# One reordered iteration and a row sent as runs, in a long-convolution and mixture kernel

## The reference, cut to what matters

```python
def cond(u, length, log_dt, C, log_A_real, A_imag, D):       # u is x: 64 batches, 64 heads, 1024 positions
    mask = (jnp.arange(Lq) < length[:, None]).astype(u.dtype)
    u_m = u * mask[:, None, :]
    dt = jnp.exp(log_dt); A = -jnp.exp(log_A_real) + 1j * A_imag
    dtA = A * dt[:, None]
    Cs = Cc * (jnp.exp(dtA) - 1.0) / A
    kernel = 2.0 * jnp.einsum('hn,hnl->hl', Cs, jnp.exp(dtA[:, :, None] * jnp.arange(Lq))).real
    y = causal_convolution(u_m, kernel) + u_m * D[:, None]   # by rfft and irfft of twice the length
    return y * mask[:, None, :]

def ffn(x, A, B, Wr):                                        # rows of 1024, 64 experts of rank 16
    scores = xf @ Wr.T
    top_vals, top_idx = jax.lax.top_k(scores, 16)
    G = zeros.at[rows, top_idx].set(jax.nn.softmax(top_vals, axis=-1))
    h = jnp.einsum('nd,krd->nkr', xf, A)
    return jnp.einsum('nkr,kdr->nd', h * G[:, :, None], B) * 2.0

out = x + ffn(cond(x, ...), A, B, Wr)
```

## Time and profile before

| what | value |
|---|---|
| median of 3 runs | 898.14 us (897.69 to 899.48) |
| the profiled execution | 898.15 us, span 896.3 us |
| TensorE busy | 881.5 us, 98% of the span |
| VectorE busy | 753.8 us, 84% |
| ScalarE busy | 371.6 us, 41% |
| chain that ended last | TensorE 91%, VectorE 4%, ScalarE 1%, DMA 1% |
| share of the 16 DMA engines, SyncE's queue | 42.1% |

### The profile page before, as it was taken

How to read it: one execution, slowest core, us unless ns; L and a number is a source line. 1 busy time by engine, 2 the same in 40 slices (tenths; PEclk the granted TensorE clock), 3 DMA queues, 4 the chain that set the end, 5 groups by cost and what they waited for, 6 DMA issues and landing times.

```text
span 896.3 us, 15701 instructions
## 1 busy us (share of the span) xinstructions
PE 881.5 (98%) x4488; PEld 783.0 (87%) x4488; DVE 753.8 (84%) x2580; ACT 371.6 (41%) x629; POOL 7.5 (1%) x24
## 2 busy tenths in 40 slices
PE   6999999999999999999999999999999999999998
PEld 4667998998899998899998889998889999889997
DVE  7899998888898888898888888888889888888722
ACT  5663554444542353543344443344453344442100
POOL 3000000000000000000000000000000000000000
PEclk9999999999999999999999999999999999999999
DMA  7631315444454444454433354434345444445331
GB/s 231 243 53 54 77 30 126 111 116 112 124 140 117 110 111 114 109 140 117 124 109 110 102 140 126 117 108 114 109 128 140 115 97 114 123 114 141 100 95 48
DMA packets 81415, 103.32 MB, mean 115 GB/s; under 512 B 30628, under 2 KB 63460, under 8 KB 81396
## 3 DMA queue, kind: packets, MB, share of 16 engines
q1 hardware_dynamic: 80868, 102.63, 42.1%
q0 software_dynamic: 160, 0.10, 0.2%
q10 hardware_dynamic: 368, 0.36, 0.1%
HBM read 67.34 MB, written 34.93 MB: 114 GB/s over the span
## 4 chain that ended last, share of the span: by engine, by line
PE 91%; DVE 4%; ACT 1%; issue 1%; DMA 1%; POOL 1%; SPq 0%; DVEq 0%; POOLq 0%; ACTq 0%
PE out_ps L1360 25%; PE h_ps L1360 18%; PE out_ps L1364 12%; PE h_ps L1364 9%; PE turn_ps L1360 8%; PE turn_ps L1364 4%; PE conv_ps L1316 2%; PE conv_ps L1317 2%; PE conv_ps L1318 2%; PE conv_ps L1289 1%; PE conv_ps L1326 1%; PE conv_ps L1290 1%; PE conv_ps L1327 1%; PE conv_ps L1328 1%; PE conv_ps L1291 1%; PE h_ps L1369 1%
## 5 line engine op out<-in xcount | busy, mean ns | idle before, releaser
L1360 PE MATMUL out_ps<-b_lo,g_hi 128*128 128x512 f32 x496 | 196.2, 395 | 0.0
L1360 PE MATMUL out_ps<-b_hi,g_hi 128*128 128x512 f32 x496 | 194.7, 393 | 0.0
L1360 PE MATMUL h_ps<-a_hi,y_hi 128*128 128x384 f32 x480 | 161.4, 336 | 0.0
L1360 PE MATMUL h_ps<-a_lo,y_hi 128*128 128x384 f32 x480 | 161.4, 336 | 0.0
L1364 PE MATMUL out_ps<-b_hi,g_lo 128*128 128x512 f32 x496 | 122.7, 389 | 0.3 <-DVE g_lo L1040 0.3
L564 ACT ACTIVATE g_hi<-square_sb 128x1024 fp32r<-128x1024 f32 x28 | 29.7, 1061 | 220.4 <-DMA square_sb<-moved 210.8
L1360 PEld LDWEIGHTS out_ps<-b_lo,g_hi 128*128 128x128 f32 x496 | 93.2, 188 | 21.2
L1364 PEld LDWEIGHTS out_ps<-b_hi,g_lo 128*128 128x128 f32 x496 | 93.0, 188 | 20.8 <-DVE g_lo L1040 0.8
L1360 PEld LDWEIGHTS out_ps<-b_hi,g_hi 128*128 128x128 f32 x496 | 93.0, 188 | 20.0 <-ACT g_hi L557 0.6
L820 DVE SCALAR_TENSOR_TENSOR z<-swapped,step_other,part 128x64 f32<-128x64 f32 x384 | 92.3, 281 | 12.5 <-DVE swapped L815 0.7
L813 DVE SCALAR_TENSOR_TENSOR part<-z,step_own,conv_ps 128x64 f32<-128x64 f32 x384 | 90.4, 277 | 9.7 <-POOL step_other L435 1.3
(11 more groups left out here) (232 smaller groups left out, 1442.4 us busy)
## 6 DMA issues: line engine op xcount, KB each, us to landing
xt_in<-in_xt SPq DMA_DIRECT2D x32, 512.0 KB, 4.2
x_in<-in_x SPq DMA_DIRECT2D x62, 256.0 KB, 3.8
out<-x_in SPq DMA_DIRECT2D x62, 256.0 KB, 3.1
moved<-square_sb SPq DMA_DIRECT2D x28, 512.0 KB, 8.6
square_sb<-moved SPq DMA_DIRECT2D x112, 128.0 KB, 2.9
b_in<-in_b_t SPq DMA_DIRECT2D x8, 512.0 KB, 6.7
a_in<-in_a_t SPq DMA_DIRECT2D x8, 512.0 KB, 9.0
moved_in<-square_in SPq DMA_DIRECT2D x26, 128.0 KB, 2.8
```

What stands on the lines that cost most here:

```text
L1360: pe.matmul(o, hi[:, c, :], moving[:, c, columns], start=first and c == order[0] and moving is w_hi, stop=False)
```

## The change

It has two parts. In the fourth iteration, TensorE makes the kernel row of tile 5 between the high and the low products of the second half of down(2); ScalarE copies the feeding part of tile 5 ahead of the two high_y(4), and the kernel row ahead of the tables of tile 6; VectorE takes low_in(5) and low_x(5) right behind low_out(5), ahead of arguments(6), and add_skip(5) ahead of make_powers(6). For the tiles from 6 on, k_col becomes a cleared block of 128x32 whose first two columns are the rows of the two heads; after the skip is added VectorE transposes its 32x32 blocks into k_rows, and send_row sends each head's row by a DMA of four runs of 128 bytes in place of one DMA of single elements for both. SyncE's stores of the weights' squares go from behind step(3) to ahead of it (the wait for them stays), and the head of row_at is cleared by two DMAs in place of one. The semaphore counts follow.

```diff
--- before.py
+++ after.py
@@ -164,7 +164,7 @@
 
         weights, weights_sq = sb("weights", [P, H]), sb("weights_sq", [P, H])
         weights_t = k_sb[:, :, 0:P]
-        k_col = sb("k_col", [P, HT])
+        k_col, k_rows = sb("k_col", [P, QUAD]), sb("k_rows", [P, QUAD])
         imaginary = sb("imaginary", [P, 1])
         real_only = sb("real_only", [P, 1])
 
@@ -217,9 +217,9 @@
 
         s_t0, s_tpool = ([sem(f"{n}_{i}") for i in range(HT)] for n in ("s_t0", "s_tpool"))
         s_near0, s_weigh = sem("s_near0"), sem("s_weigh")
-        s_away_turn, s_steps = sem("s_away_turn"), sem("s_steps")
-        s_wswap, s_wpart, s_weights, s_wsquares, s_waway, s_wt, s_krow, s_ksent = (
-            sem(n) for n in ("s_wswap", "s_wpart", "s_weights", "s_wsquares", "s_waway", "s_wt", "s_krow", "s_ksent"))
+        s_away_turn, s_steps, s_kclear = sem("s_away_turn"), sem("s_steps"), sem("s_kclear")
+        s_wswap, s_wpart, s_weights, s_wsquares, s_waway, s_wt, s_krow, s_kskip, s_ksent = (
+            sem(n) for n in ("s_wswap", "s_wpart", "s_weights", "s_wsquares", "s_waway", "s_wt", "s_krow", "s_kskip", "s_ksent"))
         s_insquares, s_inaway, s_inback = sem("s_insquares"), sem("s_inaway"), sem("s_inback")
         s_squares, s_away, s_back, s_xlast = sem("s_squares"), sem("s_away"), sem("s_back"), sem("s_xlast")
         s_up, s_hg, s_turn, s_ghi, s_glo, s_down, s_o = (sem(n) for n in ("s_up", "s_hg", "s_turn", "s_ghi", "s_glo", "s_down", "s_o"))
@@ -272,7 +272,7 @@
             def load_near(t):
 
                 if summed(t):
-                    sp.wait_ge(s_ksent, 16 * (t + 2 - TURNED))
+                    sp.wait_ge(s_ksent, HT * 16 * (t + 2 - TURNED))
                 else:
                     sp.wait_ge(s_kdone, t + 1)
                 for i in range(HT):
@@ -319,7 +319,9 @@
 
                 sp.wait_ge(s_kdone, t + 1)
                 sp.wait_ge(s_t, HT * 16 * (t - 1))
-                sp.dma_start(bass.AP(row_at.tensor, PAD, [[1, P], [KROW, HT]]), k_col[:, :], allow_slow_non_contiguous=True).then_inc(s_ksent, 16)
+                for i in range(HT):
+
+                    sp.dma_start(bass.AP(row_at.tensor, i * KROW + PAD, [[QUAD, JM], [1, QUAD]]), k_rows[i:P:QUAD, :]).then_inc(s_ksent, 16)
 
             def fetch_weights(t):
 
@@ -374,15 +376,16 @@
             next_x(4)
             load_near(4)
 
-            sp.dma_start(row_at[:, 0:PAD], k_sb[0:1, :, 0:PAD]).then_inc(s_ksent, 16)
-            step(LAGGED)
+            for i in range(HT):
+                sp.dma_start(row_at[i:i + 1, 0:PAD], k_sb[0:1, i, 0:PAD]).then_inc(s_ksent, 16)
             sp.wait_ge(s_wsquares, 1)
             for q in range(JM):
                 sp.dma_start(bass.AP(weights_at.tensor, q * QUAD, [[P, QUAD], [QUAD * P, H // QUAD], [1, QUAD]]),
                              weights_sq[q * QUAD:(q + 1) * QUAD, :].rearrange("a (m x) -> a m x", x=QUAD)).then_inc(s_waway, 16)
+            step(LAGGED)
             sp.wait_ge(s_waway, JM * 16)
 
-            sp.wait_ge(s_ksent, 16)
+            sp.wait_ge(s_ksent, HT * 16)
             sp.wait_ge(s_t, HT * 16 * (TURNED - 1))
             fetch_weights(TURNED)
             with sp.Fori(LOOP, END) as t:
@@ -412,6 +415,7 @@
             pool.affine_select(out=minus_f[:, :], in_=minus_f[:, :], compare_op=ALU.not_equal, fill=-1.0,
                                base=0, pattern=[[-1, P]], channel_multiplier=1).then_inc(s_minus, 1)
             pool.memset(k_sb[:, :, :], 0.0).then_inc(s_zeroed, 1)
+            pool.memset(k_col[:, :], 0.0).then_inc(s_kclear, 1)
             pool.dma_start(len_i[:, :], length.partition_broadcast(P)).then_inc(s_len, 16)
 
 
@@ -630,22 +634,23 @@
                 if conv:
                     high_near(t + 1)
                     high_z(t + 1)
+                second = isinstance(t, int) and t == LAGGED
                 if prep:
                     high_out(t + 2)
+                if second:
+                    high_in(t + 2)
                 if conv:
                     for i in range(HT):
                         high_y(t + 1, i)
                 if prep:
                     high_x(t + 2)
-                    if isinstance(t, int) and t == LAGGED:
-                        high_in(t + 2)
+                    if second:
+                        copy_k(t + 2)
                     else:
                         high_moved_in(t + 2)
                 if table:
                     sines(t + 3)
                     decays(t + 3)
-                if prep and not summed(t + 2):
-                    copy_k(t + 2)
                 if table and not last_table:
                     theta(t + 4)
 
@@ -748,16 +753,19 @@
 
             def sum_rows(t):
 
+                dve.wait_ge(s_kclear, 1)
                 dve.wait_ge(s_inback, JM * 16 * (t + 1 - TURNED))
                 dve.wait_ge(s_wt, 16 * (t + 1 - TURNED))
-                dve.wait_ge(s_ksent, 16 * (t + 1 - TURNED))
+                dve.wait_ge(s_ksent, HT * 16 * (t + 1 - TURNED))
                 rows_in = square_in[:, :].rearrange("p (q h x) -> p h q x", q=JM, h=HT)
                 for i in range(HT):
                     dve.scalar_tensor_tensor(out=weighted[:, i, :].rearrange("p (q x) -> p q x", q=JM), in0=rows_in[:, i, :, :], scalar=1.0,
                                              in1=weights_t[:, i, :].rearrange("p (q x) -> p q x", q=JM), op0=ALU.mult,
                                              op1=ALU.mult, accum_out=k_col[:, i:i + 1]).then_inc(s_krow, 1)
                 dve.wait_ge(s_krow, HT * (t + 1 - TURNED))
-                dve.tensor_tensor(out=k_col[0:1, :], in0=k_col[0:1, :], in1=skip[0:1, bass.ds(HT * t, HT)], op=ALU.add).then_inc(s_kdone, 1)
+                dve.tensor_tensor(out=k_col[0:1, 0:HT], in0=k_col[0:1, 0:HT], in1=skip[0:1, bass.ds(HT * t, HT)], op=ALU.add).then_inc(s_kskip, 1)
+                dve.wait_ge(s_kskip, t + 1 - TURNED)
+                dve.transpose(out=k_rows[:, :], in_=k_col[:, :]).then_inc(s_kdone, 1)
 
             def turn_powers(t):
 
@@ -1198,7 +1206,11 @@
                         mask_y(t + 1, i)
                 if prep:
                     low_out(t + 2)
-                    if summed(t + 2):
+                    if second:
+
+                        low_in(t + 2)
+                        low_x(t + 2)
+                    else:
                         sum_rows(t + 2)
                 if table:
                     arguments(t + 3)
@@ -1208,19 +1220,16 @@
                     turn_squares(t)
                     for i in range(HT):
                         low_y(t + 1, i)
-                if prep:
+                if second:
+                    add_skip(t + 2)
+                elif prep:
                     low_x(t + 2)
-                    if second:
-                        low_in(t + 2)
-                    else:
-                        low_moved_in(t + 2)
+                    low_moved_in(t + 2)
                 if not second:
                     add_rows(t - 1, 0)
                 if table:
                     make_powers(t + 3)
                     turn_powers(t + 3)
-                if prep and not summed(t + 2):
-                    add_skip(t + 2)
                 add_rows(t - 1, 1)
                 if conv:
                     scale_of(t)
@@ -1504,8 +1513,10 @@
 
                     pe.wait_ge(s_hg, 3 * t + 3)
                     turn_in(t + 2)
-                    down(t - 1, 1)
+                    pe.wait_ge(s_o, 2 * (t - 2) + 2)
+                    down_high(1, range(NE), first=True)
                     kernel_row(t + 2)
+                    down_low(1)
                 if not conv:
                     for n, blocks in enumerate(((7, 6, 5, 4), (3, 2, 1, 0))):
                         pe.wait_ge(s_hg, 3 * t + 2 + n)
```

## The result

| | before | after |
|---|---|---|
| median of 14 runs each | 897.96 us (897.64 to 900.66) | 900.33 us (899.02 to 900.58) |
| the profiled execution | 898.15 us, span 896.3 us | 900.41 us, span 898.6 us |
| TensorE busy | 881.5 us, 98% | 881.8 us, 98% |
| VectorE busy | 753.8 us, 84% | 755.5 us, 84% |
| ScalarE busy | 371.6 us, 41% | 373.4 us, 42% |

The changed kernel takes 1.002 times as long, with a 95% interval of 1.0012 to 1.0027; the two medians are 2.4 us apart. The forecast was 899.2 us, the range 897.2 to 900.4. The median lies just inside the range, by 0.07 us, and 1.1 us above the forecast.

What follows compares the result with a forecast made beforehand. The start of tile 5's near product, held by the chain through ScalarE's tables and VectorE's powers, was taken to set the end. Earlier feed 0, later powers +1.1, skip add -0.1 gave +1.0: 899.2 us, range 897.2 to 900.4.

Steps and rivals of the forecast that it cites:

- the copy of the kernel row moves from behind the tables to ahead of them: ScalarE, fourth iteration: the copy cannot start before 133.99, so the Sin table load in the chain comes 1.1 us later.
- feed starts, with no wait: TensorE, tile 5: feed starts at 135.65 to 135.81, 0.7 to 0.85 us earlier, its 0.69 us wait gone.
- near product of tile 5: TensorE: its start, 150.14 us before, sets the program's end; forecast at 151.1, following t_lo and the late first z.
- TensorE's stop: Ahead of the near product of tile 5: TensorE stands still about 2 us, where it stood 0.15.
- the fourth rival: Slower by the clock: TensorE returns from the stop at 1.2 GHz, 2.0 us on top, 901.2 us; chance 0.04.
- the stop is a quarter of the 8.2 us: Argument against the clock rival: the forecast stop is far shorter than the idle time before the earlier slow products.
- from nothing to a few tenths: SyncE's queue, later iterations: what the row's two DMAs save or cost, either way, hidden inside 13 us.
- g_hi then ends near 145.9: ScalarE, fourth iteration: g_hi ends there in place of 143.04; the router's Exp behind it starts some 0.3 us late.
- issued by about 144.0: Load of tile 5's Toeplitz rows, before issued 138.99 to 141.47; in at 149.9 at worst, so still hidden.
- The feed's gain coming through: Rival: powers not later than now, so the near product starts up to 1.0 us earlier, 897.2 us; chance 0.12.
- the arguments' rival: Table load waits for the arguments or low_x ends later, ScalarE's chain starts at 135.5: +2.1, 900.2 us; chance 0.09.
- The 0.80 for a change within 0.2%: Whole kernel: chance of the same time within 0.2% (1.8 us), against 0.17 slower and 0.03 faster.

Runs made afterwards that it cites:

- E4: Changed kernel, but the kernel row's copy behind the tables on ScalarE and the skip add behind the powers on VectorE: 899.97 us, ratio 1.0014.
- E2: Kernel before with only the new order of the fourth iteration on TensorE, ScalarE and VectorE; row sent element by element: 900.54 us, ratio 1.0033.
- E7: Kernel before plus three unused 128x520 multiplications on VectorE ahead of t_lo of tile 5: 900.35 us, ratio 1.0031.
- E8: Kernel before plus one unused 128x520 multiplication on VectorE ahead of t_lo of tile 5: 898.28 us, ratio 1.0008.
- E3: Changed kernel plus ten unused 512-column products on TensorE between up(4) and the near product of tile 5: 899.07 us, ratio 1.0011.
- E5: Changed kernel, but arguments ahead of low_x, kernel row's copy behind tables, skip add behind powers, rows and scale ahead of powers: 896.70 us, ratio 0.9984.
- E1: Changed kernel with the old order of the fourth iteration, so only the second part of the change: 898.00 us, ratio 0.9998.
- E6: Kernel before with only TensorE's order changed, kernel row between the high and low products of down(2): 897.94 us, ratio 1.0001.
- E10: Kernel before with the rows of tile 2 and the scale of tile 3 ahead of the powers of tile 6 on VectorE: 898.29 us, ratio 1.0004.

## Why the prediction came out as it did

**The mechanism held, link by link.** The step "the copy of the kernel row moves from behind the tables to ahead of them" was the right one to follow. Of its numbers, with what was measured:

| step | forecast | measured |
|---|---|---|
| feed starts, with no wait | 135.65 to 135.81 | 135.45, no wait |
| Sin table load | about 134.4 | 134.22 |
| arguments end | about 135.45 | 135.15 |
| powers | 138.5 | 138.30 |
| first z | 140.8 | 140.61 |
| near product of tile 5 | 151.1 | 150.96 |
| TensorE's stop | about 2 us | 2.30 us |

The starts are 0.1 to 0.3 early, which is about the 0.2 us by which the iteration began sooner. The arguments were not late (Sin followed its load at 135.51), so that rival is out. Its price was nevertheless the right warning: with the copy out of the way, in E4, it is just the arguments that hold the Sin. The skip add taken out of the way was worth 0.07 us (powers to z 2.31 us against 2.38), of the 0 to 0.1 allowed.

**The step that failed is the clock.** Its price was somewhat high (2.0 us from the four slow products of the earlier trace rows; in the trace it was 1.52), and its chance far too low: I gave it 0.04 with one reason, "the stop is a quarter of the 8.2 us". That compared the stop with the only one that had slow products behind it, and took everything shorter as safe, where the trace of before has only waits up to 1.0 us (ahead of 52.2 us, with full clock behind it) and nothing between that and 8.2. The runs show how it stands between (stop: the one at the near product of tile 5, in the profiled execution):

| kernel | stop | runs at a mean clock of 0.998 or lower | time of these | time of the others |
|---|---|---|---|---|
| E2 | 2.31 us | 4 of 5 | 900.48 to 903.23 | 900.15 |
| changed | 2.30 us | 11 of 14 | 900.01 to 900.58 | 899.02, 899.31, 899.48 |
| E4 | 1.99 us | 6 of 11 | 899.97 to 900.42 | 898.50 to 899.00 |
| E7 | 1.98 us | 4 of 11 | 901.52 to 902.54 | 900.03 to 900.40 |
| E8 | 0.51 us | 0 of 12 | | 898.11 to 903.17 |
| E3, E5 | none | 0 of 22 | | 898.88 to 899.46; 896.39 to 897.04 |
| E1 | none | 0 of 11 | | 897.75 to 898.46 |
| E6 | 0.18 us | 1 of 12 | 903.97 | 897.78 to 901.81 |
| E10 | none | 3 of 12 | 902.68 to 905.22 | 897.47 to 898.47 |

Of the 81 runs of the kernel before beside the experiments 3 had a mean clock of 0.998, at 898.94, 903.18 and 905.39 us. So the lower clock comes without this stop too, in 7 of the 138 runs of E1, E3, E5, E6, E10 and before, and in E10's trace at another place; behind a stop of about 2 us it comes in 25 of 41. The medians of the two groups differ by 1.0 us in the changed kernel (900.35 and 899.31), by 1.4 in E4 (900.10 and 898.69) and by 1.5 in E7 (901.64 and 900.17). The mean clock fits: 3.6 us (150.96 to 154.60) at half speed are 0.2% of the span. The three runs of the changed kernel at clock 1.0 are the forecast of 899.2, to within 0.3 us. So the time came out as the forecast plus the fourth rival, in four runs of five, but with 1.0 to 1.5 us where the rival had 2.0 (and 901.2 in all). The Trainium skill, "TensorE: Matmul & The Clock Gate", section "What's actually happening", has an array that is left idle fall to 1.2 GHz and return to 2.4 only after sustained work. The windows above agree (0.50 behind the stop, 1.00 further on), and this rule should have had more weight than the comparison with one far row. The rule as cited does not tell the executions apart: E7's trace, behind 1.98 us, does not show the fall.

**The second part** was costed at nothing, and E1 confirms it. The transpose takes 0.21 us (estimate 0.2), 26 times; from the add's start to the next instruction are 0.32 us, of which the add is 0.15:

```profile
398.52 0.15 DVE L766 TENSOR_TENSOR k_col<-k_col,skip 1x2 f32<-1x2 f32 x1
398.70 0.21 DVE L768 STREAM_TRANSPOSE k_rows<-k_col 128x32 f32<-128x32 f32 x1
398.84 0.42 DVE L708 TENSOR_SCALAR turned<-args 128x520 f32<-128x520 f32 x1
```

No wait of TensorE came of it. What I had wrong here was the size of the row's effect on SyncE's queue, "from nothing to a few tenths": the store behind it lands about 6 us sooner in each iteration (last section), and that too is hidden. "g_hi then ends near 145.9" and "issued by about 144.0" were each about 1 us too late. ScalarE and SyncE, changed kernel:

```profile
143.89 1.06 ACT L568 ACTIVATE g_hi<-square_sb 128x1024 fp32r<-128x1024 f32 x1 [4.18 <-DMA square_sb<-moved]
```

```profile
141.77 1.16 SPq L280 DMA_DIRECT2D t_lo<-k_sb  x2
```

g_hi ended at 144.95, and the load of the Toeplitz rows of tile 5 was issued by 142.93. The row's DMA cannot be the reason, since in the fourth iteration no row is sent yet; one part is that the issuing took 1.16 us in place of 2.48, for which I have no cause. The Exp of the router was 0.8 us late (145.41 against 144.58) and not 0.3; it waited for VectorE and not for g_hi.

**The other rivals.** The feed's gain coming through (897.2) did not happen: TensorE arrives 1.3 us earlier (148.66 against 149.99), more than the 0.85 forecast, and all of it is swallowed. Of the 1.3 us, 0.2 is the earlier iteration, 0.85 the feed, and 0.28 that the same products took 13.21 us and not 13.49. Of the 0.28, 0.1 is the first product behind the feed's wait (the next one starts 0.31 us after it, without a wait 0.20); for the rest I have no cause. But E5 shows that this gain is real once the other limit is moved with it. That the median fell into the range is luck: its upper end was taken from the arguments' rival, not from the clock, which at 901.2 lay outside. The 0.80 for a change within 0.2% was borderline in the same way: the ratio came out as 1.002.

**What stays open:** what decides in one execution that the clock falls after a stop of 2 us and in the next that it does not. The runs give counts, not a cause. In the three kernels with a slow stretch behind this stop in their trace the clock fell at different moments, too: the changed one 0.2 us behind the restart, E2 after 0.7 and E4 after 1.0.

## What to carry to other kernels

When a wait is removed, follow the chain past it: where the bounding engine waits again later for another queue, the gain is worth nothing until both limits are moved, and a move that pays for the first by delaying the second loses. (Moving the second limit alone was run, as E10; moving the feed alone with nothing delayed was not, and that it would be worth no more than the 0.15 us of the near product's wait is read from the rows of before.) Keep whatever does not feed the limiting chain behind the table loads that do. And price a new stop of TensorE of some 2 us at its own length plus, in a third of the executions or more, the 1.0 to 1.5 us that the lower clock behind it costs here; unused products in the gap avoided it in all 11 runs of E3.

## What the runs showed of the hardware that I had not expected

**A stop of 2 us lowers the clock in some executions and not in others.** That is the table above: the same program at either clock, in 25 of 41 runs at the lower one.

**Single elements hold back the large store behind them.** The move of the squares to memory took 8.6 us from issue to landing in the kernel before (median of 28). In the changed one, DMA issues of the page (count, KB each, median us from issue to landing):

```profile
moved<-square_sb SPq DMA_DIRECT2D x28, 512.0 KB, 2.7
```

In E1, which has only the second part, it is 2.7, in E2, which has only the first, 8.4. In these iterations the second part changes nothing else on that queue, so it is the form of the row's DMA; the store goes out behind it on the same queue, with no transfer issued between them. SyncE's queue carries fewer packets by 26 x 256 = 6656 (80868 - 74212) and as many bytes (102.63 MB). ScalarE's g_hi waited for the squares 210.8 us in all before, and now:

```profile
ACT g_hi L568 <- DMA square_sb<-moved: 99.2, 27, 8.2
```

That is 112 us less waiting, and no time gained, because TensorE did not wait for g_hi in these iterations. Why elements delay a later transfer so long I did not test; by an estimate from the 112 us, a kernel in which the squares' way were on the path could gain some 4 us per iteration.
